# Cross-attention and LoRA feed-forward on one core: other numbers of scores in the quarters of even steps, and an earlier inverse in odd steps

## The reference, cut to what matters

```
x = x + attention(layernorm(x), ctx, ctx)      # keys = values = ctx
    scores  = q k^T / sqrt(32)
    weights = softmax(scores)
    out     = weights v
x = x + ffn(layernorm(x), ...)
    gates of 8 experts from projections of x; per row the largest gate selects
    one expert's low-rank update (rank 8), bias and debias; the result is
    (1 - gate) * x + gate * (bias + degen(update(x - debias)))
```

## Time and profile before

| | |
|---|---|
| median of 3 runs | 1004.49 us (1004.46 to 1005.07) |
| the profiled execution | 1002.18 us |
| its span in the trace | 1000.4 us |
| TensorE busy | 933.3 us (93%) |
| VectorE (DVE) busy | 901.6 us (90%) |
| ScalarE (ACT) busy | 721.8 us (72%) |
| GpSimd (POOL) busy | 799.6 us (80%) |
| granted TensorE clock | 0.998 of full speed |

### The profile page before, as it was taken

The page is one execution under the profiler, slowest core; times in us unless marked ns, Lnnn a source line. Parts: engine busy times, 40 slices in busy tenths (PEclk is TensorE's granted clock), DMA queues, the critical chain, the costliest instruction groups (busy, mean ns, idle before and its releaser), DMA issues.

```text
span 1000.4 us, 24586 instructions
## 1 busy us (share of the span) xinstructions
PE 933.3 (93%) x9518; PEld 375.5 (38%) x9518; DVE 901.6 (90%) x1106; ACT 721.8 (72%) x1301; POOL 799.6 (80%) x454
## 2 busy tenths in 40 slices
PE   4789999999999999999999999999999899999996
PEld 3223333333333333333333333333222226777773
DVE  6989999999999999999999999988888876889976
ACT  5388888888888888888888888887777776554540
POOL 7269999999999999999999999999999998222110
PEclk9999999999999999999999999999999999999999
DMA  7876676868686868585858586857556653866324
GB/s 252 214 176 160 137 183 142 190 139 193 131 193 132 189 134 199 125 199 126 199 128 200 130 196 131 191 106 170 114 128 150 154 112 115 265 213 229 147 106 168
DMA packets 319875, 164.18 MB, mean 164 GB/s; under 512 B 182216, under 2 KB 307240, under 8 KB 319760
## 3 DMA queue, kind: packets, MB, share of 16 engines
q1 hardware_dynamic: 319456, 161.76, 65.8%
q0 software_dynamic: 304, 0.85, 0.4%
HBM read 107.58 MB, written 54.53 MB: 162 GB/s over the span
## 4 chain that ended last, share of the span: by engine, by line
PE 65%; DVE 21%; issue 11%; ACT 1%; POOL 1%; DMA 0%; SPq 0%; DVEq 0%; ACTq 0%; POOLq 0%
PE psum L588 18%; PE psum L602 15%; DVE row_max L923 11%; PE psum L550 8%; PE psum L615 6%; PE psum L733 5%; PE psum L576 4%; PE psum L711 4%; PE psum L625 2%; DVE den_t L935 2%; DVE probs L1134 2%; PE psum L699 2%; PE psum L633 1%; DVE row_max L914 1%; DVE o_t L929 1%
## 5 line engine op out<-in xcount | busy, mean ns | idle before, releaser
L862 ACT ACTIVATE probs<-psum 128x512 f32<-128x512 f32 x1024 | 553.0, 596 | 136.2 <-PE psum L588 121.1
L923 DVE TENSOR_REDUCE row_max<-psum 128x4 f32<-128x2048 f32 x248 | 565.2, 2279 | 49.8 <-PE psum L550 49.4
L588 PE MATMUL psum<-q_stack,k_stack 97*32 97x512 f16 x4096 | 332.8, 385 | 5.4 <-ACT probs L862 2.0
L363 POOL TENSOR_TENSOR sums<-probs 128x2048 f32<-128x2048 f32 x63 | 287.9, 4570 | 13.4 <-ACT probs L862 13.3
L351 POOL TENSOR_TENSOR sums<-probs 128x2048 f32<-128x2048 f32 x63 | 287.0, 4555 | 9.3 <-ACT probs L862 9.3
L602 PE MATMUL psum<-probs,v_in 128*32 128x512 f32 x2048 | 267.3, 596 | 3.9
L588 PEld LDWEIGHTS psum<-q_stack,k_stack 97*32 97x32 f16 x4096 | 96.7, 94 | 252.3 <-ACT probs L862 164.8
L550 PE MATMUL psum<-high_mem 32*128 32x512 f16 x992 | 98.0, 384 | 24.7 <-DVE row_max L923 21.1
L602 PEld LDWEIGHTS psum<-probs,v_in 128*32 128x32 f32 x2048 | 58.3, 109 | 83.4 <-issue 54.2
L328 POOL TENSOR_TENSOR o_all<-o_all,o_t 128x512 f32<-128x512 f32 x64 | 81.6, 1275 | 9.2
L323 POOL TENSOR_TENSOR o_t<-o_t,inv 128x512 f32<-128x512 f32 x64 | 67.4, 1053 | 25.1 <-DVE inv L941 25.1
(11 more groups left out here) (119 smaller groups left out, 765.5 us busy)
## 6 DMA issues: line engine op xcount, KB each, us to landing
q_stack<-q_split SPq DMA_DIRECT2D x192, 128.0 KB, 3.4
xa<-in_x_dram SPq DMA_DIRECT2D x32, 512.0 KB, 3.7
o_all<-in_x_dram SPq DMA_DIRECT2D x256, 64.0 KB, 2.4
x_attended<-o_all SPq DMA_DIRECT2D x64, 256.0 KB, 4.6
out_dram<-probs SPq DMA_DIRECT2D x32, 512.0 KB, 2.9
q_split<-prod_mem SPq DMA_DIRECT2D x15, 1024.0 KB, 5.6
xa<-x_attended SPq DMA_DIRECT2D x16, 512.0 KB, 4.5
probs<-x_attended SPq DMA_DIRECT2D x16, 512.0 KB, 4.8
```

The lines of the kernel that those rows point to most:

```text
L363: pool.tensor_tensor(sums[:, 2 * u % SUMS], probs[:, u % 2, 0], probs[:, u % 2, 1], ALU.add).then_inc(front_done, 1)
L588: last = pe.matmul(st_ps[row:row + D, bank_of["score", u, n], :], k_stack[:, u % SLOTS, t * P + row:t * P + row + D], q_stack[:, u % SLOTS ...
L862: act.activation(probs[:, s, keys, g, :], st_ps[:, bank_of["score", u, n], :], ACT.Exp, scale=EXP_SCALE).then_inc(exped, 1)
L923: dve.reduce_max(row_max[:, u % 2, t:G * ST:ST], s_ps[:], AX.X).then_inc(reduced, 1)
```

## The change: what it does

Three edits:

1. In even steps the four quarters take 5, 5, 3 and 3 scores; they took 4, 5, 4 and 3. The product with v stands after the second score of quarters 1 and 2 (as before), and in quarter 0 after the third.
2. In quarter 0 of an even step the three scores ahead of the product are split: two, then `last_denominators(u-2)`, then one more, then the product with v, then two.
3. On VectorE, `invert(u-2)` of an odd step moves from quarter 1 (behind that quarter's `low_part`, ahead of the reduction of quarter 2) to the head of quarter 0's work behind its reduction, ahead of `low_part` and `take_rows`. In even steps it stays.

```diff
-            BEGIN = ((0, 4, 9, 13, NSC), (0, 4, 8, 12, NSC))
-            MIDST = ((2, 6, 11, 15), (2, 6, 10, 14))
-            NORM_AT = 13
+            BEGIN = ((0, 5, 10, 13, NSC), (0, 4, 8, 12, NSC))
+            MIDST = ((3, 7, 12, 15), (2, 6, 10, 14))
+            NORM_AT, HALVES_AT = 13, 2
...
+                        halves = t == 0 and live(u - 2) and u % 2 == 0 and u < UNITS
                         if live(u):
-                            score_keys(u, BEGIN[u % 2][t], MIDST[u % 2][t])
+                            score_keys(u, BEGIN[u % 2][t], HALVES_AT if halves else MIDST[u % 2][t])
...
-                        if t == 0 and live(u - 2) and u % 2 == 0 and u < UNITS:
+                        if halves:
                             last_denominators(u - 2)
+                            score_keys(u, HALVES_AT, MIDST[u % 2][t])
...
+                        if t == 0 and live(u - 2) and u % 2 == 1:
+                            invert(u - 2)
                         if late and t < PIECES:
                             low_part(n, t)
...
-                        if t == 1 and live(u - 2):
+                        if t == 1 and live(u - 2) and u % 2 == 0:
                             invert(u - 2)
```

## The result

The changed kernel takes 1011.53 us (median of 7 runs, 1008.59 to 1014.46), the kernel before on the same chips 1004.49 (7 runs, 1002.40 to 1006.00). The ratio is 1.0073, interval 1.0058 to 1.0087: slower by 7.0 us, small but clear of the noise, where the forecast was 10 us slower (1014.5 us, which the 1011.53 lie 3 us under). The profiled execution took 1011.16 us, with a span of 1009.4 and a clock of 0.995; before it was 1002.18, 1000.4 and 0.998.

The account below looks back on a forecast made before the run. No single engine bounds; TensorE and VectorE share the chain. 30 even steps at +0.18 and 30 odd at +0.16 gave +10.2, kept as +10 over 1004.49: 1014.5 us; own range 1010.5 to 1017.5, wider range 1002.0 to 1017.0.

Parts of the forecast that it names:

- the bank: Even-step quarter 0: fifth score gets the denominators' bank, waits for den_taken and delays L550 of quarter 1; +0.35 us.
- the score out of quarter 2: Even-step quarter 2, held by TensorE: one score less gains time; -0.17 us, ends -0.22 and 0.
- Even step: The two score edits of an even step together: +0.35 - 0.17 = +0.18 us.
- the inverse: Odd-step quarter 0: moved inverse delays L975, o_t and the reduction of quarter 1; +0.16 us, ends -0.11 and +0.25.
- The low end of the term, −0.11: Odd steps: the inverse's old place gives its cost back and the new place is hidden; -0.11 us.
- The forecast's sum: 30 even steps at 0.18 and 30 odd steps at 0.16: +10.2 us, kept as +10, giving 1014.5 us.
- Only the inverse costs: Rival: even steps come out even, only the odd-step inverse adds 4.8 us; 1009.3 us, chance 0.22.
- faster: Rival: quarter 2's gain stays, quarter 0's fifth score delays no reduction; 997.9 us, or 1002.7 with inverse's cost; chance 0.15.
- the split at 0: Even-step quarter 0: score between denominators and product only starts ScalarE's exponential earlier, outside this chain; 0 us.
- GpSimd: Odd steps: GpSimd's 25.1 us wait for the inverse goes, but nobody waits for GpSimd; no value.
- the port: Rival: odd-step inverse excluded by GpSimd's sum for 3.0 us each, +90 us; about 1095 us, chance 0.02.

Follow-up runs that it names:

- e5: New scores and split, old inverse, planner keeping even units' denominators' bank one use longer (KEPT den 6, 5), against the kernel before: 1001.85 us, ratio 0.9969.
- e7: New scores and split, old inverse, KEPT den 7, 6 so no fifth score takes the denominators' bank, against the kernel before: 998.00 us, ratio 0.9946.
- e2: The kernel before with only the odd-step inverse moved to the head of quarter 0's work: 1008.67 us, ratio 1.0038.
- e8: The kernel before with the odd-step inverse moved later, to the end of quarter 2 behind low_part: 1007.79 us, ratio 1.0041.
- e1: The changed kernel with the inverse back in its old place, so new scores and split only: 1008.64 us, ratio 1.0035 against the kernel before.
- e3: e1 without the split: in quarter 0 three scores, then denominators, then product with v: 1014.94 us, ratio 1.0123 against the kernel before.
- e9: e1 with even-step quarters of 4, 6, 3, 3 scores, keeping the split of quarter 0: 994.60 us, ratio 0.9907 against the kernel before.
- e4: The kernel before with even-step quarters of 4, 6, 3, 3 scores, without the split: 1001.99 us, ratio 0.9968.
- e12: The e9 kernel repeated in another session: 993.91 us, ratio 0.9890 against the kernel before.

## Why the prediction was right, and where it was off

- **Right, the bank.** The fifth score waits for `den_taken` ahead of L550. L550 of quarter 0 to L550 of quarter 2 went from 6.28 to 6.64 (420.17 to 426.81), +0.36 against +0.35 predicted. Each part is there: 0.33 from the score to L550, and a reduction that waits 0.24. e5 and e7 tie it to the bank.
- **Right in sign, too small: the score out of quarter 2.** Predicted −0.17, measured −0.24 from L550 to L550 (3.39 to 3.15), which is outside the ends I had given it (−0.22 and 0). I had taken 0.05 off because the second score would wait for an exponential. It stands 0.27 us behind the first in the changed kernel (402.37 to 402.64), where it was 0.29 before, so this term has the other sign: −0.02. A likely reason is that everything in quarter 2 now comes later by 0.36, which gives the exponential time: e7, the same scores without that delay, has 0.35 between the two (423.24 to 423.59). But from step 54 on e7 has no delay either, and its second score does not wait at all, so the banks of the scores ahead count as well, and the reason is not shown by itself. Even step: +0.12 instead of +0.18.
- **Mis-sized, the inverse.** Predicted +0.16 per odd step, measured +0.10. The 0.16 from its start to the next instruction's is right in the new place too (410.38 to 410.54). But L977 behind it took 0.28 to the next start (410.54 to 410.82), where L975 took 0.33 before (406.92 to 407.25). That is not peculiar to L977: in the late pairs `o_t` stands right behind the inverse, and its own 0.63 to the next start (776.15 to 776.78 before) is 0.58 in e2 (758.01 to 758.59). So the instruction behind the inverse gives 0.05 back at once, whichever it is; why, the traces don't say. I had taken the price of the inverse from its own pitch alone. The low end of the term, −0.11, stood for something else, a gain from the old place; e8 shows that this place had cost next to nothing.
- **The forecast's sum.** 30 × (0.18 + 0.16) = 10.2 was predicted. With the measured terms it is 30 × (0.12 + 0.10) = 6.6, with terms that are not rounded 6.73, and the stretch says 7.04. The rest is 0.31: I had left out quarter 0 of step 62, which still waits for the bank (3.75 us instead of 3.44) and is the 31st in the stretch. Without it e1 would cost 3.59. Both terms erred to the same side, the sign and the range held. The profiled executions are 9.0 us apart, near my 10, but that nearness is luck: 1.9 of it lies outside the stretch. "Only the inverse costs" (1009.3) is refuted by e1, "faster" by the quarter of 3.75 us.
- **Wrong, the split at 0.** I had said that it only lets ScalarE start earlier and that ScalarE is not in the chain. e3 shows 7.87 us against e1. The argument looked at what the moved score itself delays, and not at what stands behind its wait: the denominators, for which `den_t` and through it the fifth score and L550 wait, and the product with v, for which `o_t` waits. And ScalarE's earlier start is not worth nothing either: e9 against e4 shows 5.40 us (8.49 − 3.09), by way of an exponential that quarter 2 waits for. The mistake did not touch the forecast, since the change had the split in it and the working was done on rows without that wait. But it would have made a forecast of e3 wrong by 8 us.
- **Right with a limit, GpSimd.** It gained its wait for the inverse and nobody profited. The limit is e8: the lateness is free in the steps, not at the hand-over.
- **Refuted, the port.** In the changed kernel the inverse at 410.38 lies inside a sum of GpSimd (408.86 to 413.45), and took 0.24 us; 31 of the 64 lie wholly inside an instruction of GpSimd. All inverses of the changed kernel (durations in ns, minimum, median, maximum):

```profile
L943 DVE RECIPROCAL inv<-den_t x64: 203/243/245, 76.9 to 851.4; 128x16 f32<-128x16 f32 x64
```

None was held, so the 1095 us of that rival did not come. The Trainium skill, page "SBUF — State Buffer", section "Who interferes with whom", also says that a VectorE instruction with at most one SBUF input, outside the two-port modes, does not contend with GpSimd. The inverse reads one tensor, `den_t`, and the trace agrees with that: 203 to 245 ns for all 64. Which port mode it ran in, no row here shows.

What stays open: why the instruction behind the inverse has a shorter pitch, and what sets the distance of the first two scores in quarter 2 of the changed kernel.

## What to carry to other kernels

Ask of every instruction that takes a buffer from a rotating pool who held it last, and what stands behind the wait on its engine: here the same distribution of work cost 3.9 us or gained 5.3 by which bank one score got. A wait is priced by what is queued behind it and by who waits for that, not by the work that waits, and an engine's slack must be followed to the end of the phase, because the next phase may collect it. Where a step is full, give work to the quarter whose loop has room *behind* the critical issue (quarter 1 in e9), not ahead of it.

## What the runs showed of the hardware

- **The clock near the end differs from run to run.** The ten us that end 10 us before the end of the program, by the table of stretches, for the kernel before, the changed one and e12 (start:end, length, busy PE, PEld, DVE, ACT, POOL, clock, DMA):

```profile
980.40:990.40 10.00, 6.85 (x16) 2.92 (x15) 7.36 (x30) 0.83 (x2) 0.00 (x0) 0.83 0.32 131
```

```profile
989.40:999.40 10.00, 6.86 (x13) 2.81 (x12) 6.78 (x27) 0.83 (x2) 0.00 (x0) 0.69 0.25 105
```

```profile
972.10:982.10 10.00, 6.85 (x23) 3.24 (x22) 8.72 (x34) 0.83 (x2) 0.00 (x0) 1.00 0.22 89
```

  In the 40 us ahead of it the clock was 1.00 in all three, and TensorE was busy for over 19 of each 20 us. TensorE's busy time is the same in the three rows, and the granted clock, a mean over the stretch, was 0.83, 0.69 and 1.00. From the last layer norm instruction of ScalarE (L835, L837 in the others) to the end it took 74.1, 75.4 and 72.5 us, longer where the clock was lower. So of the 1.5 us that the changed kernel's execution is longer behind the stretch, 1.3 lie there. The runs of the changed kernel lie 6 us apart; the fastest (1008.59) had a mean clock of 1.000 and the slowest (1014.46) 0.994, so the dip is a likely part of that spread. The stretch is the sharper measure: e9 and e12, the same kernel, agree in it to 0.02 us. What sets off the dip was not tried.
- **A score ahead of row scores costs 0.33 us, one ahead of L615 0.22.** The changed kernel shows both for the same four matmuls: 423.59 to 423.92 ahead of L550 (timeline), and 428.88 to 429.10 ahead of L615 (chain).
- **The costs of single places add almost exactly:** e1 and e2 sum to 6.93 of 7.04, and in the pair of the table the quarters that an edit doesn't touch keep their length to 0.03 us in ten kernels.
